# Projections one group earlier, and a gate that fills four banks, in a delta-rule attention layer with a mixture of experts

## The reference, cut to what matters

```python
q, k, v = (short_conv(x @ W.T, conv_w) for W, conv_w in ...)      # 4 taps, then silu
beta = sigmoid(x @ Wb.T)
# delta rule per head in chunks: A = -tril(k*beta @ k.T), T = (I - A)^-1, u = T v, w = T (k*beta)
#   u_i = u_i - w_i S;  o = q_i S + tril(q_i k_i.T) u_i;  S = S + k_i.T u_i
short, long = fir(v, 3 taps), fir(v, 63 taps)
paths = (short, long, delta, v)
gate_in = concat([x] + [mean and variance of each path per head])
hmid = gelu(gate_in @ gate_w1.T + gate_b1)                          # 512 hidden
probs = softmax((hmid @ gate_w2.T + base_bias) / temp), floored, normalised
out = rmsnorm(sum(probs * paths)) @ Wo.T
x = layernorm(x + out)
x = layernorm(x + top-2 of 8 experts(x))
```

## Time and profile before

| | |
|---|---|
| median of 3 runs | 1892.97 us (1891.18 to 1901.68) |
| the profiled execution | 1894.72 us |
| its span, first to last instruction | 1893.0 us |
| mean granted clock of TensorE | 0.904 |
| PE busy | 1496.2 us, 79% of the span |
| DVE busy | 1315.3 us, 69% |
| ACT busy | 950.1 us, 50% |
| POOL busy | 440.7 us, 23% |

### The profile page before, as it was taken

One profiled execution on the slowest core, in us unless ns is written; L12 is line 12 of the kernel. 1 busy time (PEld: TensorE's weight loads), 2 busy tenths in 40 slices (PEclk: granted clock), 3 DMA queues, 4 the chain that ended last, 5 costly groups with the idle time before them and its releaser, 6 DMA issues. The chain is left out here.

```text
span 1893.0 us, 40332 instructions
## 1 busy us (share of the span) xinstructions
PE 1496.2 (79%) x12507; PEld 1108.8 (59%) x12508; DVE 1315.3 (69%) x3331; ACT 950.1 (50%) x1998; POOL 440.7 (23%) x473
## 2 busy tenths in 40 slices
PE   6775165979999999999999999887436999999800
PEld 3445134747747747657557567476225888888700
DVE  6995155677787887887887887875455555554488
ACT  6772061356555644654655555542443555555434
POOL 6884200000030040040030210300223333333300
PEclk9997585989999999999999999998758999999955
DMA  5558642023243243333333333232524533333295
GB/s 197 190 163 256 154 101 58 3 67 94 71 127 92 62 122 102 78 91 101 87 89 106 95 106 90 79 97 76 196 91 140 192 105 101 104 104 101 77 385 190
DMA packets 297370, 224.34 MB, mean 119 GB/s; under 512 B 173472, under 2 KB 265632, under 8 KB 296960
## 3 DMA queue, kind: packets, MB, share of 16 engines
q1 hardware_dynamic: 225600, 158.84, 29.0%
q0 software_dynamic: 15232, 43.53, 6.4%
q10 hardware_dynamic: 56384, 19.93, 4.1%
HBM read 130.42 MB, written 91.82 MB: 117 GB/s over the span
## 5 line engine op out<-in xcount | busy, mean ns | idle before, releaser
L1462 DVE SCALAR_TENSOR_TENSOR B_conv<-B_ps_x,B_cw,B_conv 128x511 f32<-128x511 f32 (+2 forms) x192 | 143.5, 748 | 65.9 <-ACT B_conv L1176 59.3
L2031 POOL DMA_INDIRECT y_d<-C_yb,C_dest x136 | 132.1, 971 | 232.0 <-ACT C_yb L2142 229.7
L422 POOL DMA_INDIRECT xs_d<-x,slot_u x128 | 133.4, 1042 | 137.4 <-DVE m_acc L1857 100.6
L688 POOL MEMSET B_z<- 128x256 f32 (+4 forms) x40 | 5.5, 191 | 674.6 <-DMA B_z<-scr_a 674.6
L1176 ACT ACTIVATE B_conv<-B_ps_x,B_cw 128x512 f32<-128x512 f32 x64 | 43.7, 683 | 167.6 <-PE B_ps_x L745 167.3
L2261 DVE TENSOR_TENSOR C_av<-C_sg,C_ps_g 128x256 f32<-128x256 f32 x136 | 57.3, 421 | 94.6 <-ACT C_sg L2136 94.6
L2065 PE MATMUL C_ps_g<-C_w_high,C_xt_high 128*128 x272 | 119.5, 439 | 0.4 <-issue 0.4
L745 PE MATMUL B_ps_x<-B_xa,B_wk 128*128 128x512 f32 x128 | 67.5, 655 | 63.8 <-DVE B_sel L1454 44.9
L2273 DVE TENSOR_TENSOR C_avt_low<-C_ps_a,C_avt_high 128x256 fp32r<-128x256 f32 x136 | 57.7, 425 | 83.5 <-ACT C_avt_high L2131 83.5
L2065 PE MATMUL C_ps_g<-C_w_high,C_xt_low 128*128 x272 | 107.7, 396 | 0.0
L2065 PE MATMUL C_ps_g<-C_w_low,C_xt_high 128*128 x272 | 107.0, 393 | 0.0
(11 more groups left out here) (330 smaller groups left out, 4250.6 us busy)
## 6 DMA issues: line engine op xcount, KB each, us to landing
C_xb<-xs_d SPq DMA_DIRECT2D x136, 132.0 KB, 2.1
C_w_high<-y_d SPq DMA_DIRECT2D x12, 1024.0 KB, 14.1
A_band<-fir_long POOLq DMA_DIRECT2D x32, 256.0 KB, 5.9
A_work<-xT SPq DMA_DIRECT2D x16, 512.0 KB, 5.0
v_d<-A_v_tok SPq DMA_DIRECT2D x16, 512.0 KB, 3.5
short_d<-A_sh_tok SPq DMA_DIRECT2D x16, 512.0 KB, 3.2
B_xa<-xT SPq DMA_DIRECT2D x8, 1024.0 KB, 5.8
B_v_tok<-v_d SPq DMA_DIRECT2D x8, 1024.0 KB, 5.5
```

The source lines that it names most:

```text
L422: pool.indirect_dma_start(t["xs_d"][:, :], bass.IndirectOffsetOnAxis(ap=slot_u[:, c:c + 1], axis=0), x1[:, b, j, :], None).then_inc(done, 16)
L1462: V.scalar_tensor_tensor(conv[:, g % 2, k:], X[g % 2][:, :SEQ - k], cw[:, g // 4, gg % CH, 3 - k:4 - k], conv[:, g % 2, k:], ALU.mult, ALU ...
L2031: pool.indirect_dma_start(t["y_d"][:, :], bass.IndirectOffsetOnAxis(ap=dest[:, q:q + 1], axis=0), yb[:, u], None).then_inc(y_out[u], 16)
```

## The change

Seven things are changed at once.

1. *Key groups 1 and 2 move up into the merging*: `project(i + 1, 1)` and `(i + 1, 2)` stand where two fills stood (2 and 3 units); in the recurrence groups 3, 4, 5 take the place of 2, 3, 4. ScalarE takes group 1's first tap in `merge_and_mix`, VectorE its taps first thing in `recur`, before `state(0)`.
2. *Query group 5 moves up* from `stage1b` into the recurrence's last step; its taps follow VectorE's `residual(3)`, and group 4's taps move ahead of `residual(3)`.
3. *Group 0 of the pair after the next* is projected at the end of `step`, ahead of a fill that shrinks from 4 units to 2, no longer behind the wait for the solver's store.
4. *The gate uses four banks* (`hidden = (X[0], X[1], B3, B4)`). The part of the first sequence that needs no statistics (`from_x`) moves up into `stage1b`, in the place of the fills between `select(5)`, `select(6)` and `select(7)`: four blocks of two matmuls of 512 columns. The statistics' part (`from_stats`) follows in `gate`.
5. *Fills*: 7 units fewer in `stage1b` (9 before, 2 after, on B5), 5 fewer in `merges`, 2 fewer at the end of `step`.
6. *`mask_at`* waits for VectorE's third weighing operation in place of the `mt` DMAs.
7. *VectorE's statistics of the values* (`bn(q, 2)`) are spread over the start of the recurrence.

TensorE's part of the diff, and what else is spoken of (the waits on the other engines follow the same moves):

```diff
+        hidden = (X[0], X[1], B3, B4)
...
                     pool.wait_ge(at_kept, 8 * (p + 1))
-                    pool.wait_ge(mt_in[1], 32 * (p + 1))
+                    need(pool, mixd, 4 * (p - 1) + 1)
...
+                def from_x(i, b, c):
+                    pe.wait_ge(xg_in[b], 16 * (i + 1))
+                    for k in range(CH):
+                        mm(hidden[c][:], w1x[:, k, c * P:(c + 1) * P], xg[b][:, k, :], start=k == 0, stop=False)
+
+                def from_stats(c):
+                    mm(hidden[c][:], w1s[:, c * P:(c + 1) * P], st_t[:], start=False, stop=True).then_inc(gate_mm, 1)
...
                     turn_norms(p, 0)
-                    project(p, 5)
...
-                    for g in range(5, 8):
-                        select(p, g)
-                        if last is not None:
-                            if g == 5:
-                                pe.wait_ge(a_kept[1], 4 * (p + 1))
-                            spin(B3, 2)
+                    if first:
+                        for g in range(5, 8):
+                            select(p, g)
+                    else:
+                        select(p, 5)
+                        for k in a_kept:
+                            pe.wait_ge(k, 4 * (p + 1))
+                        from_x(p - 1, 0, 2)
+                        select(p, 6)
+                        from_x(p - 1, 0, 3)
+                        pe.wait_ge(taps, 24 * p + 21)
+                        from_x(p - 1, 0, 0)
+                        pe.wait_ge(taps, 24 * (p + 1))
+                        from_x(p - 1, 0, 1)
+                        select(p, 7)
+                        spin(B5, 2)
                     turn_norms(p, 1)
                     if last is not None:
                         rank(last)
-                        spin(B3, 3)
...
-                    if has_prev:
-                        spin(X[1], 2)
+                    if has_next:
+                        project(i + 1, 1)
...
-                    if has_prev:
-                        spin(X[1], 3)
+                    if has_next:
+                        project(i + 1, 2)
...
-                    if has_next:
-                        project(i + 1, 1)
...
-                            project(i + 1, s + 1)
+                            project(i + 1, s + 2)
...
+                def gate(i, has_prev, has_next):
...
+                    turn_stats(i, 0)
...
+                    for c in range(HID_CH):
+                        from_stats(c)
+                    turn_stats(i, 1)
+                    for c in range(2):
+                        pe.wait_ge(gelu_ok, 8 * i + c + 1)
+                        from_x(i, 1, c)
...
+                    logits(i, 0)
+                    pe.wait_ge(st_kept, 2 * i + 2)
+                    for c in range(2):
+                        from_stats(c)
+                    for c in range(2, HID_CH):
+                        from_x(i, 1, c)
+                        from_stats(c)
+                    pe.wait_ge(raw_kept, 2 * i + 1)
+                    logits(i, 1)
...
-                    if has_next:
-                        hold(pe, x_out, 16 * (i + 1))
-                        project(i + 1, 0)
                     merges(i, has_prev, has_next)
...
                         at_rest(i + 1)
-                        spin(X[1], 4)
+                    if has_after:
+                        project(i + 2, 0)
+                        spin(X[1], 2)
...
-                    for q in range(TPB):
-                        bn(q, 2)
+                    if has_next:
+                        taps_of(i + 1, 1)
+                    bn(0, 2)
                     state(0)
-                    if has_next:
-                        taps_of(i + 1, 1)
+                    bn(1, 2)
                     output(0)
...
                     output(2)
+                    if has_next:
+                        taps_of(i + 1, 4)
 
                     residual(3)
...
                     if has_next:
-                        taps_of(i + 1, 4)
+                        taps_of(i + 1, 5)
```

More of the change, by code:

```diff
@@ L809, in at_products, with stage1b @@
                                 i.then_inc(at_mm, 1)
-                def stage1b(p, last=None):
+                def from_x(i, b, c):
[4 more added lines that the diff above has]
+                    mm(hidden[c][:], w1s[:, c * P:(c + 1) * P], st_t[:], start=False, stop=True).then_inc(gate_mm, 1)
+                def stage1b(p, last=None, first=False):
                     if last is not None:
@@ L996, in recur, with turn_stats @@
                         within(i, s)
[L998 to L1002, removed]
+                def turn_stats(i, b):
                     for j in range(TPB):
@@ L1006, in gate, with logits @@
                     w.then_inc(st_turned, 1)
-                    pe.wait_ge(xg_in[b], 16 * (i + 1))
+                def logits(i, b):
+                    pe.wait_ge(gelu_ok, 8 * i + 4 * (b + 1))
                     for c in range(HID_CH):
[L1009 to L1022, removed]
+                        w = mm(B2[c * LANE:(c + 1) * LANE, :], w2[:, c, :], hid[:, c, :], start=True, stop=True)
+                    w.then_inc(raw_mm, 1)
+                def gate(i, has_prev, has_next):
+                    if has_prev:
+                        pe.wait_ge(rt, RT * (i - 1) + 1)
+                    pe.wait_ge(st_dve, ST * (i + 1))
+                    turn_stats(i, 0)
+                    if not has_next:
+                        pe.wait_ge(taps, 24 * (i + 1))
+                        for c in range(HID_CH):
+                            from_x(i, 0, c)
+                    pe.wait_ge(st_kept, 2 * i + 1)
+                    for c in range(HID_CH):
+                        from_stats(c)
[4 more added lines that the diff above has]
+                    if has_next:
                         for k in a_kept:
@@ L1107, in _ @@
                 turn_betas(0)
-                for g in range(1, 5):
+                for g in range(1, 6):
                     project(0, g)
@@ L1111, in _, with step @@
                         select(0, g - 2)
-                select(0, 3)
-                stage1b(0)
+                stage1b(0, first=True)
                 at_first(0)
                 at_rest(0)
-                def step(i, has_prev, has_next):
-                    if has_next:
-                        hold(pe, x_out, 16 * (i + 1))
-                        project(i + 1, 0)
+                project(1, 0)
+                def step(i, has_prev, has_next, has_after):
                     merges(i, has_prev, has_next)
@@ L1133, in step @@
                         rank(i - 1)
-                    for b in range(2):
-                        gate(i, b, has_prev, has_next)
+                    gate(i, has_prev, has_next)
                     if has_next:
@@ L1311, in recur, with gate, keep_stats @@
                             keep_x1(i - 1, 1)
[L1313 to L1323 removed]
+                def gate(i):
+                    def keep_stats(b):
+                        act.wait_ge(st_turned, 2 * i + b + 1)
+                        need(act, gate_mm, 8 * i + 4 * b)
+                        A(st_t[:], TR[0:3 * STATS, :], ACT.Copy).then_inc(st_kept, 1)
+                    keep_stats(0)
+                    for b in range(2):
+                        need(act, raw_mm, 2 * i + b)
+                        for c in range(HID_CH):
+                            act.wait_ge(gate_mm, 8 * i + 4 * b + c + 1)
+                            A(hid[:, c, :], hidden[c][:], ACT.Gelu, bias=b1[:, c:c + 1]).then_inc(gelu_ok, 1)
+                        if b == 0:
+                            keep_stats(1)
+                        act.wait_ge(raw_mm, 2 * i + b + 1)
+                        A(raw_logits[:, b, :], B2[:], ACT.Copy).then_inc(raw_kept, 1)
                 def rms(i, b):
@@ L1401, in _ @@
                 load_solved(0)
-                for k in range(5):
+                for k in range(3):
+                    merge(0, k)
+                group_a(1, 1)
+                for k in range(3, 5):
                     merge(0, k)
@@ L1410, in step @@
                         keep_routes(i - 1)
-                    for b in range(2):
-                        gate(i, b)
+                    gate(i)
                     A(warm[:], eps5[:], ACT.Exp)
@@ L1857, in place @@
                     V.tensor_tensor(m_acc[:], m_acc[:], m_sum[:], ALU.add).then_inc(rt, 1)
-                for g in range(5):
+                for g in range(6):
                     taps_of(0, g)
```

36 lines of the change are left out of this document (13 added, 23 removed).

## The result

The changed kernel takes 1929.35 us, median of four runs (1927.47 to 1932.98), against 1893.07 us (1891.18 to 1901.68): a ratio of 1.0185, 95% interval 1.0151 to 1.0219. The forecast was 15 us slower (1908 us), with a range up to 1922; measured are 36. The profiled executions differ by 1925.7 - 1893.0 = 32.7 us of span, and that is split up here.

The account below looks back on a forecast made before the run. VectorE's chain was taken to bound the loop from the keys to the merging's end, TensorE the recurrence. Terms summed to +2.45 us a pass, +14.7 over six passes: 1908 us median, range 1880 to 1922.

Parts of the forecast that it names:

- (a): Query norms: from_x blocks ahead of select(7) delay it and VectorE's query norm; +2.85 us a pass.
- (b): Recurrence: TensorE's stall for the residual add goes, as VectorE takes group one's taps earlier; -1.1 us a pass.
- (c): Key stage: project(5) and its taps leave, but key copies still wait in turn; -0.1 us a pass.
- (e): Start of the recurrence, solve_rows to to_state: slower with TensorE's clock down from the start; +1.1 us a pass.
- VectorE's three losses: Behind the solver: waits for logits (0.67 us) and first tap (1.45), a slow addition (1.1) go; -3.2 us together.
- (d): Behind the solver: idle TensorE awaits mt, merges partly at half clock, leaving little of VectorE's gain; -0.3 us a pass.
- E: Time mark in each pass: the end of the solver's transposed copy; mt was forecast at about E + 6.5.
- pair 0 and pass 0 taken at nothing: First pass, last pass and the part before the loop: taken at 0, within 5 us on either side.

Follow-up runs that it names:

- e5: The changed kernel with the four from_x blocks moved behind the query norms and two fills behind each of the three selections; ratio 0.9957 to the kernel before.
- e6: The changed kernel with three fills added ahead of solve_rows(i, 0); ratio 1.0092 to the kernel before.
- e1: The changed kernel with the four from_x blocks moved from between the selections to behind the query norms and the rank; ratio 1.0057 to the kernel before.
- e10: The changed kernel with the store of the solver's transposed copy cut in four, the needed half first; ratio 1.0130 to the kernel before.
- e11: The changed kernel with 13 in place of 2 fills at the end of a step, ahead of the merging; ratio 1.0126 to the kernel before.
- e14: The changed kernel with pair 0's mask, and no other, waiting for the mt loads again as before the change; 1919.88 us in one run.
- e12: The kernel before the change with two fills added ahead of solve_rows(i, 0); ratio 0.9957 to the kernel before.
- e2: The changed kernel with nine in place of two fills at the end of each step, ahead of the merging; ratio 1.0110 to the kernel before.

## Why the prediction was too low

**Right.** (a): +3.3 measured for +2.85, and e5 gives it back by order alone (norm 7.2 us behind `select(5)`). (b) and (c): -1.3 for -1.2, and project_out no longer waits for the add. (e): +0.99 for +1.1, and e6 shows that it is the clock. That the size fits so well is in part luck: 7.40 us is what the stretch takes at 0.50 throughout (four passes of e1, three of e5), and the change ran at 0.53 to 0.60 (6.97); but 6.3, the mean of five passes, was set against it for six, whose mean is 5.98. VectorE's three losses in (d) are gone as forecast. The kind of loss in (d) was right too: an idle TensorE, half clock, a second product that VectorE waits for. In pass 5, where the store was not disturbed, that product stood at E + 17.5, the forecast place, and the loss was 0.1 us.

**Wrong: the arrival of `mt` in (d).** "At about E + 6.5" was worked out from one pass, in which the store took 2.8 us, and from a landing of 3.1 us. Measured are E + 7.1 to 10.2, mean 8.9. In four of six passes the store took 4.5 to 5.1 us. The wait ends with the second of SP's two loads, which took 3.9 us to land (3.8 before; the 3.1 is the median of both): even before the change it landed at E + 6.7 to 8.9. At half clock this goes through to `solve_rows` in full: passes 1 to 4 start the product 2.3 us later than passes 5 and 6, and lose 2.3 us each behind E against the kernel before, passes 5 and 6 nothing. So (d) is +1.52 in place of -0.3, 10.9 us in six passes. The warning stood in the trace of before: there the store took 3.9, 3.9 and 4.9 us in three of eight solves. It cost nothing in two of them, since TensorE came later than `mt`, and a wait of 0.72 us in the third; the change took that cover away, and I gave the arrival no upper bound of its own, and (d) as a whole one of only +1 us. e10 and e11 take the two factors apart: an earlier `mt` at half clock won 1.7 us in passes 1 to 4, full clock with as late a product 3.2 us.

**Wrong: pair 0 and pass 0 taken at nothing.** The mask no longer waits for `mt`. I followed that into the loop, where it frees VectorE's addition, but not into pair 0, where it falls on the solver: 3.65 us (e14). From pair 0's first projection to its query norm it took 1.55 us more, with project(0, 5) now ahead of the key norms; that this is the cause is not shown, since in e12, with the order of before, it took 1.15 us more as well. Pass 0 pays (a) in full (3.7 us), 2.5 us net. With 0.9 us behind the loop, 1.7 us less in the stage ahead and 0.9 less in pair 0's merging that is 6.0 us for a forecast of 0 (bounded by 5).

The forecast of 14.7 us, 10.9, 6.0 and some 1.1 us of the sizes of (a), (b), (c) and (e) make the 32.7.

The Trainium skill, page "SBUF — State Buffer", section "SBUF: two separate sides", says that VectorE and GpSimd share one pair of ports as an exclusive lock, held for a whole instruction, against VectorE operations with two SBUF inputs. The traces agree: 4.04 us for 0.39, ending 0.2 us behind the mask, and before the change L1725's 2.35 us for 1.23, which began under a mask. Applied to the moved wait, it would have named pair 0's loss.

## What to carry to other kernels

Work that fills a gap does two things, and moving it opens two holes: look where it came from, for the clock, and where it goes, for who queues behind it. A transfer that was covered has an arrival of its own: before taking the cover away, read it over all passes, and bound it by the worst. A wait that is dropped lets its instruction run earlier everywhere, also in the first pass: see what runs beside it there.

## What was not expected of the hardware

In passes 1 to 6 of the change a store of 512 KB took 2.7 to 2.8 us, but 4.4 to 5.1 us when a packet of the instruction queue (16 KB) lay in its time. The transfers in 6 us around pass 4's two stores (1 MB), and in 4 us around pass 5's second store (rates in 40 slices):

```profile
GB/s 254 0 0 0 0 0 0 355 519 382 410 410 355 410 410 355 382 410 410 410 410 410 410 273 0 27 27 27 27 27 27 27 27 27 27 27 0 27 27 27
...
q8 instruction: 1, 0.02, 2.0%
...
GB/s 41 492 410 369 532 410 328 532 410 369 451 451 369 410 369 492 410 328 532 451 328 532 410 369 451 246 0 0 10 90 159 175 157 206 218 196 112 92 127 131
```

In pass 4 the stores are through after 2.4 us, but for a rest that goes on at 27 GB/s, about a sixteenth of the rate; in pass 5 there is no such rest and no such packet. ScalarE's loads start 1.7 us behind the start of the rest, so they are not its cause. That the packet is, was only seen beside it, not tried; but in the fourteen traces in which the store is one, 33 stores with such a packet starting between 0.5 us ahead of them and 1.9 us behind their start took 3.9 to 5.3 us, and 72 without one between 1.5 us ahead and 1.9 us behind took 2.6 to 3.3 us.

The clock also fell without one long wait: in e1 to 0.50 behind waits of 1.70 and 1.92 us with 0.43 us of small products between them, and in e2 a wait of 1.90 us behind 7.9 us of fills gave a product of 3.00 us, while in e1 waits of 1.6 to 2.1 us ahead of the same product left it at 2.21 in three passes.
